# First steps reordered by hand on all engines, and the first turn of each unit with half the transposes and silu in four half-height operations

## What is computed

```python
# sandwich: x = x + layernorm(A(layernorm(x)));  x = x + layernorm(B(layernorm(x)))
h = x @ Win.T + bin                                  # 512 -> 64
for l in range(4):                                   # A: four layers on 64 features
    y = silu(layernorm(h, l1w, l1b))
    h = h + sconv(y, phazor, last_conv) * scl        # decaying complex convolution over the sequence
    y = silu(layernorm(h, l2w, l2b) @ w1.T + b1)     # 64 -> 256
    h = h + y @ w2.T + b2                            # 256 -> 64
out = layernorm(h) @ Wout.T + bout
# B: hidden + gate * (softmax over the 8 best of 128 memory slots) @ values ..., with
#    router scores (+ log_rel), a learned and a variance-based uncertainty for the gate
```

## Time and profile before

| | us |
|---|---|
| median of 3 runs | 204.45 (204.21 to 204.62) |
| the profiled execution | 204.57 |
| its span | 202.8 |
| mean granted clock of PE | 0.992 of full speed |
| HBM read, written | 10.87 MB, 4.19 MB |

### The profile page before, as it was taken

One profiled execution on the slowest core, in us unless ns is written; L12 is line 12 of the kernel. 1 busy time (PEld: TensorE's weight loads), 2 busy tenths in 40 slices (PEclk: granted clock), 3 DMA queues, 4 the chain that ended last, 5 costly groups with the idle time before them and its releaser, 6 DMA issues.

```text
span 202.8 us, 3759 instructions
## 1 busy us (share of the span) xinstructions
PE 181.9 (90%) x1210; PEld 148.8 (73%) x1210; DVE 157.4 (78%) x547; ACT 109.8 (54%) x281; POOL 84.0 (41%) x142
## 2 busy tenths in 40 slices
PE   0797996859999998999999899999999898988992
PEld 0797995758988788788998689989988444555430
DVE  6898978886588768784977776655899997998872
ACT  1595687524456467637555445462836585863210
POOL 4222269724044422343224522467462735555400
PEclk9999999978999999999999999999999999999999
DMA  5999990000000000000000000000000000002675
GB/s 158 419 376 400 417 368 14 5 0 0 0 5 0 0 3 0 0 3 0 0 0 5 0 0 0 3 0 3 2 0 2 0 3 0 2 0 105 228 283 216
DMA packets 5505, 15.31 MB, mean 75 GB/s; under 512 B 925, under 2 KB 1965, under 8 KB 4462
## 3 DMA queue, kind: packets, MB, share of 16 engines
q1 hardware_dynamic: 5486, 15.07, 19.7%
HBM read 10.87 MB, written 4.19 MB: 74 GB/s over the span
## 4 chain that ended last, share of the span: by engine, by line
PE 68%; DVE 7%; POOL 7%; DMA 6%; ACT 5%; issue 3%; SPq 2%; DVEq 0%; ACTq 0%
PE bank L1508 15%; PE bank L1400 11%; PE bank L1632 7%; PE bank L1490 6%; DMA M<-in_mraw 6%; PE bank L1464 4%; PE bank L1452 4%; POOL RS L360 4%; PE bank L1567 3%; PE bank L1638 3%; POOL M L380 2%; PE bank L1440 2%; PE bank L1556 2%; ACT XA L593 2%; DVE Z L1001 1%
## 5 line engine op out<-in xcount | busy, mean ns | idle before, releaser
L360 POOL TENSOR_TENSOR RS<-SS,nhalf 128x4 f32<-128x4 f32 x36 | 42.9, 1202 | 67.9 <-DVE SS L995 67.6
L1508 PE MATMUL bank<-ffst,HD 128*128 128x128 f32 x256 | 32.7, 283 | 0.0
L1508 PEld LDWEIGHTS bank<-ffst,HD 128*128 128x128 f32 x256 | 31.3, 200 | 0.2
L995 DVE TENSOR_REDUCE SS<-SQ 128x4 f32<-128x260 f32 x36 | 15.2, 421 | 20.9 <-ACT SQ L635 20.3
L1400 PE MATMUL bank<-M,XT 128*128 128x226 f32 x128 | 27.6, 362 | 0.1
L659 ACT ACTIVATE HD<-bank,b1r 128x512 f32<-128x512 f32 x32 | 20.3, 684 | 10.9 <-PE bank L1490 10.8
L1400 PEld LDWEIGHTS bank<-M,XT 128*128 128x128 f32 x128 | 23.2, 189 | 3.6 <-issue 3.1
L635 ACT ACTIVATE SQ<-bank 128x256 f32<-128x256 f32 x36 | 13.8, 383 | 19.6 <-PE bank L1508 9.6
L640 ACT ACTIVATE Y<-bank,cvst 128x512 f32<-128x512 f32 x16 | 12.5, 779 | 15.1 <-PE bank L1452 15.1
L1035 DVE TENSOR_TENSOR_SCAN V<-cvst,U 128x514 f32<-128x514 f32 x16 | 19.5, 1218 | 0.0
L1490 PE MATMUL bank<-Z,w1r 64*128 64x256 f32 x128 | 18.1, 402 | 0.4
(11 more groups left out here) (265 smaller groups left out, 346.0 us busy)
## 6 DMA issues: line engine op xcount, KB each, us to landing
...
```

The lines of the kernel that those rows point to most:

```text
L360: pool.tensor_tensor(RS[:, g, :], SS[:, g, :], nhalf[:, :], ALU.pow).then_inc(done, 1)
L995: dve.tensor_reduce(SS[:, g, :], SQ[:, g, :, :], AX.X, ALU.add).then_inc(done, 1)
L1508: last = pe.matmul(HK[g][:, j * P:(j + 1) * P], HD[:, u % 2, a, at:at + P], ffst[:, L, a * P:(a + 1) * P], start=False, stop=True, skip_gr ...
```

## The change

It has two parts. First, the order of the first steps is written out anew on POOL, ACT, DVE and PE (each has now a `first_steps`). SP issues chp first, c6 ahead of XT(0), and w2r behind X(2) instead of ahead of M. PE computes nine products of `ones` with itself into a spare bank before the first real one and three after it (`warm`). chp's first operations on DVE come ahead of the wait for winr. mix_columns comes behind turn1(0), setup_ffn behind column_sums; project_x(0) and (1) have banks of their own and come before hidden(0). project(0) adds b2 from the f32 row B2F at its start, where it took B2W at its end. score_rows is cut in two and moved ahead of the sums of steps 13 and 14. In setup_late(1) eight PE records (four products) become one transpose.

Second, from unit 4 to unit 15 DVE writes each tile's features once (scale in place of scale_twice, 256 columns), turn1 makes two transposes instead of four, each of two tiles side by side, and silu1 is four operations of 64 partitions x 256 columns: each half of the partitions of T1B is written to both halves of Y.

```diff
-        XPAIR = {ts[0]: ts for ts in XSTEP.values() if len(ts) == 2}
+        XPAIR = {ts[0]: ts for k, ts in XSTEP.items() if len(ts) == 2 and k >= 3}
...
         def x_bank(t):
+            if t < 2:
+                return bank[6 + t][:, 0:XW]
             at = HW if t in XSECOND else 0
             return LB[:, at:at + XW]
...
+            sp.dma_start(chp[:, :], ch).then_inc(s_ch, 16)
             sp.dma_start(winr[:, :, :], win).then_inc(s_win, 16)
             sp.dma_start(binr[:, :], binb).then_inc(s_win, 16)
-            sp.dma_start(chp[:, :], ch).then_inc(s_ch, 16)
+            sp.dma_start(c6[:, :], c64).then_inc(s_c64, 16)
...
-                if g == 0:
-                    sp.dma_start(c6[:, :], c64).then_inc(s_c64, 16)
                 if g == 1:
                     sp.dma_start(WOR[:, :], woutb).then_inc(s_m, 16)
+                    sp.dma_start(M[:, :, 0:AW], mraw).then_inc(s_m, 16)
+                if g == 2:
                     sp.dma_start(w2r[:, :], w2n).then_inc(s_w2, 16)
-                    sp.dma_start(M[:, :, 0:AW], mraw).then_inc(s_m, 16)
...
-                if s < GROUPS:
-                    norm(s, ss1, rs1)
-                if s == 2:
-                    for c in range(1, VC):
-                        centre_m(c)
-                if s + 1 < GROUPS:
-                    input_rstd(s + 1)
-                if s == 1:
-                    centre_m(0)
+            def first_steps():
+                norm(0, ss1, rs1)
+                input_rstd(1)
+                norm(1, ss1, rs1)
+                centre_m(0)
+                input_rstd(2)
+                centre_m(1)
+                norm(2, ss1, rs1)
+                centre_m(2)
+                centre_m(3)
+                input_rstd(3)
+                norm(0, ss2, rs2)
+                norm(3, ss1, rs1)
+                norm(1, ss2, rs2)
+                norm(4, ss1, rs1)
+                norm(2, ss2, rs2)
...
-            for s in range(UNITS + 1):
+            first_steps()
+            for s in range(GROUPS, UNITS + 1):
                 step(s)
...
             def silu1(u):
                 g, L = u % GROUPS, u // GROUPS
                 act.wait_ge(t1, u + 1)
-                act.activation(by_seq(Y[:, g, :])[:, :, 1:SL], by_seq(T1B[:, :]), ACT.Silu,
-                               bias=cvst[:, L, LB0:LB0 + 1], scale=cvst[:, L, LW0:LW0 + 1]).then_inc(y1, 1)
+                if u < GROUPS:
+                    act.activation(by_seq(Y[:, g, :])[:, :, 1:SL], by_seq(T1B[:, :]), ACT.Silu,
+                                   bias=cvst[:, L, LB0:LB0 + 1], scale=cvst[:, L, LW0:LW0 + 1]).then_inc(y1, 1)
+                    return
+                for lo in (0, DIM):
+                    for to in (0, DIM):
+                        at = 1 + lo // DIM * P
+                        last = act.activation(by_seq(Y[to:to + DIM, g, :])[:, :, at:at + P],
+                                              by_seq(T1B[lo:lo + DIM, 0:HW]), ACT.Silu,
+                                              bias=cvst[lo:lo + DIM, L, LB0:LB0 + 1],
+                                              scale=cvst[lo:lo + DIM, L, LW0:LW0 + 1])
+                last.then_inc(y1, 1)
...
+            def first_steps():
+                square(0, (h0_done, 1), sq1)
+                input_mean(1)
+                input_squares(GT, 2 * GT)
+                mix_rows()
+                silu1(0)
+                square(1, (h0_done, 2), sq1)
+                input_mean(2)
+                input_squares(2 * GT, 2 * GT + 2)
+                column_means()
+                input_squares(2 * GT + 2, 3 * GT)
+                silu1(1)
+                ffn_out()
+                square(2, (h0_done, 3), sq1)
+                input_mean(3)
+                input_squares(3 * GT, 3 * GT + 2)
+                square(0, (a1, 1), sq2)
+                input_squares(3 * GT + 2, 4 * GT)
+                silu1(2)
+                x_out(0)
+                square(3, (h0_done, 4), sq1)
+                x_out(1)
+                z_out(0)
+                square(1, (a1, 2), sq2)
+                silu2(0, 0)
+                silu2(0, 1)
+                silu1(3)
+                square(4, (a2, 1), sq1)
+                z_out(1)
+                square(2, (a1, 3), sq2)
+                silu2(1, 0)
+                silu2(1, 1)
...
             def step(s):
-                if s < GROUPS:
-                    square(s, (h0_done, s + 1), sq1)
                 ffn = 0 <= s - 2 < UNITS
-                if s + 1 < GROUPS:
-                    input_mean(s + 1)
-                    if s < 2:
-                        input_squares((s + 1) * GT, (s + 2) * GT)
-                if s == 1:
-                    square(0, (a1, 1), sq2)
-                if s == 2:
-                    input_squares(3 * GT, 3 * GT + 2)
-                    z_out(0)
-                    input_squares(3 * GT + 2, 4 * GT)
-                    square(1, (a1, 2), sq2)
                 if s < UNITS:
                     silu1(s)
                 else:
                     last_z(s)
-                if s == 0:
-                    ffn_out()
-                if s == 1:
-                    column_means()
-                if s >= 3:
-                    for t in XSTEP.get(s - 1, ()):
-                        x_out(t)
+                for t in XSTEP.get(s - 1, ()):
+                    x_out(t)
                 if GROUPS <= s + 1 < STEPS:
                     if 2 * GROUPS <= s + 1 < 3 * GROUPS:
                         pads_out(s + 1 - 2 * GROUPS, s - GROUPS + 2)
                     square(s + 1, (a2, s - GROUPS + 2), sq1)
-                if ffn and s >= 3:
+                if ffn:
                     z_out(s - 2)
-                if 2 <= s - 1 < UNITS:
+                if 0 <= s - 1 < UNITS:
                     square(s - 1, (a1, s), sq2)
                 if ffn:
                     silu2(s - 2, 0)
...
+            def mark(ins):
+                chain[0] += 1
+                ins.then_inc(dve_step, 1)
...
+            dve.wait_ge(s_ch, 16)
+            dve.tensor_scalar(pol[:, 0, :], chc("re"), -1.0, None, ALU.mult)
+            link(dve.tensor_scalar(pol[:, 1, :], chc("im"), -1.0, None, ALU.mult))
+            dve.tensor_tensor(pol[:, 2, :], pol[:, 0, :], chc("re"), ALU.max)
+            mark(dve.tensor_tensor(pol[:, 3, :], pol[:, 1, :], chc("im"), ALU.max))
+            mark(dve.tensor_tensor(pol[:, 4, :], pol[:, 2, :], pol[:, 3, :], ALU.max))
+            mark(dve.tensor_scalar(pol[:, 5, :], pol[:, 4, :], TINY, None, ALU.max))
...
-                link(dve.scalar_tensor_tensor(out=B2F[:, :, :], in0=rows(sm[0:ROWS, 32:32 + DEPTH], DEPTH, DIM),
-                                              scalar=-1.0 / DIM, in1=b2r[0:ROWS, :, :], op0=ALU.mult, op1=ALU.add))
+                dve.scalar_tensor_tensor(out=B2F[:, :, :], in0=rows(sm[0:ROWS, 32:32 + DEPTH], DEPTH, DIM),
+                                         scalar=-1.0 / DIM, in1=b2r[0:ROWS, :, :], op0=ALU.mult,
+                                         op1=ALU.add).then_inc(b2_mean, 1)
+                dve.wait_ge(b2_mean, 1)
                 link(dve.tensor_copy(B2W[:, :, :], B2F[:, :, :]))
...
+            def score_rests():
...
-                table_level(4, 0, 1)
+                table_level(0, 0, DEPTH)
+                table_level(1, 0, DEPTH)
+                first_h(0)
+                table_level(2, 0, DEPTH)
                 sum_squares(0, sq1, ss1)
-                table_level(5, 0, 1)
+                table_level(3, 0, DEPTH)
                 scale_twice(0)
-                table_level(6, 0, 1)
-                table_level(7, 0, 1)
+                for k in range(4, 8):
+                    table_level(k, 0, 1)
+                first_h(1)
                 modulate(0)
-                first_h(1)
-                scan(0)
                 sum_squares(1, sq1, ss1)
-                demodulate(0)
                 table_level(4, 1, 2)
                 scale_twice(1)
-                table_level(5, 1, 2)
-                sum_squares(0, sq2, ss2)
+                scan(0)
+                demodulate(0)
                 modulate(1)
                 first_h(2)
+                sum_squares(2, sq1, ss1)
+                table_level(5, 1, 2)
+                scale_twice(2)
                 scan(1)
-                sum_squares(2, sq1, ss1)
+                demodulate(1)
+                sum_squares(0, sq2, ss2)
+                ffn_means()
+                first_h(3)
                 scale(0, rs2, z2)
-                demodulate(1)
-                scale_twice(2)
-                ffn_means()
+                modulate(2)
+                sum_squares(3, sq1, ss1)
+                scale_twice(3)
                 sum_squares(1, sq2, ss2)
-                first_h(3)
-                modulate(2)
+                scan(2)
                 scale(1, rs2, z2)
-                sum_squares(3, sq1, ss1)
-                scan(2)
-                scale_twice(3)
                 demodulate(2)
```

(59 more changed lines are left out.)

24 lines of the change are left out of this document (8 added, 16 removed).

## The result

The changed kernel takes **212.44 us** (median of 4 runs, 210.25 to 212.66) against 204.33 for the kernel before beside it: ratio **1.0365, 95% interval 1.0328 to 1.0401**. It is slower by 8 us, where 199.1 was forecast with a range to 202.4. The steps are compared in stretches of profiled executions in which that clock reads 1.00.

The account below looks back on a forecast made before the run. PE (TensorE), 90% busy, was taken to bound most steps, a chain over ACT, POOL and DVE the filling. Gains of 2.7 (filling) and 2.65 us (steps) sum to 5.35, giving 199.1 us; 8-in-10 range 196.8 to 202.4.

Parts of the forecast that it names:

- With 0.10 overlap 0.46 each: silu1 in the twelve steps: four half-height operations on ScalarE take 0.46 us net each, 1.84 in all.
- the filling: Stretch before the twelve steps: the new order brings turn1(4) to 49.4 us, a gain of 2.7 us.
- Hidden at 3.40: Within a step, T being turn1's start: hidden starts 3.40 us after T, behind z_out, against 3.53 before.
- Rival 2: Twelve steps: ACT becomes their bound, silus of 0.52 to 0.55 or later x_outs; +2.8, 201.9 us; chance 13%.
- Rival 3: Twelve steps: half-height silus cost 0.68 net, deciding from 0.57 us per operation; +10.6, 209.8 us; chance 6%.
- Step 13: score_rows goes before the sum, removing PE's stall ahead of turn1(14): -0.9 and -0.3, together -1.2 us.
- Step 7: Bound by the loop from project round to turn1, from which 0.29 + 0.22 go: -0.5 us.
- Step 5: Transpose of vpT replaces eight records of 1.08 us: about -0.9; the loop allows it, at T + 5.13.
- (a): Start of the kernel: first_h(0) at 7.7 to 11.3 us, first_h(1) ends at 16.7 instead of 17.5, 0.7 gained.
- (b): From first_h(2) to turn1(3): turn1(3) at 41.3 us, or 40.8 with POOL undisturbed, instead of 42.65.
- (c): Around turn1(3) to turn1(4): PE's clock holds, project(0) takes 1.8 instead of 3.35 us; waiting on silu2(0) loses 0.6 to 0.9.
- Rival 1: Early first steps: PE's clock falls in a new gap and slows first_h(2), +2 to 2.3 us, 201.3 us; chance 12%.

Follow-up runs that it names:

- the first part alone: The kernel before with only the new order of the first steps, the moved score_rows and the transpose in setup_late(1): 203.2 us, ratio 0.9943.
- after: The whole changed kernel, both parts, against the kernel before: 212.44 us, ratio 1.0365.
- two silus: The changed kernel with the two of four half-height silus that write the other half of Y left out: 201.36 us, ratio 0.9817 to the kernel before.
- gaps filled: Twelve unread products in PE's two new idle times before turn1(0): added to the changed kernel 210.48 us; added to its first part without the second 201.47 us.

## Why the prediction was wrong, step by step

**"With 0.10 overlap 0.46 each" (the steps): the overlap was wrong.** The duration was right (0.56), the overlap of 0.10 was carried over from z_out without its condition. The text even named the gap ("No row shows an ACT operation that reads one half of the partitions and writes the other") but then asked only how much of the *duration* is fixed, while the overlap was taken as given; its sign of being wrong, too, looked at the 0.56 alone. Four silus take 2.30 us, not 1.84, so hidden is later by about 0.47. By the prediction's own threshold of 0.57 net, 0.575 an operation, with the filling's 2.7 us gained, would have been about break-even with before, not a loss of 8 us. The rest is the next step.

**"Hidden at 3.40", counted from T: a wait was missing.** The list of what PE waits for in a step had z_out and not x_out. turn2(u) writes a bank from which x_out still has to read (its wait is on xa_read), and x_out stands behind the silus. Before, x_out was done at T + 1.66 and turn2 came at T + 2.33 without an idle time, so nothing showed it; PE's timeline of before, T being 97.03:

```profile
99.36 0.38 PE L1477 MATMUL bank<-ident,Z 128*128 128x128 f32 x2
```

With the silus as forecast, x_out would have ended at T + 2.62, turn2 come at about 2.75 and hidden, 1.24 later, at T + 3.99: 0.59 of the error is this wait alone, 0.48 the missing overlap, and 3.40 + 0.59 + 0.48 = 4.47 is what was measured. The split between the two is reckoned; what a run shows is that putting x_out first gave 0.68 a step back, and 4.5 us of the 10.2 by which all steps missed. By the same account the step with x_out breaks even with before where 0.42 + 4n + 0.37 + 0.13 + 1.24 = 3.53, at n = 0.34 us an operation, and not at 0.57: an estimate, since other waits would come in.

**Rivals 2 and 3.** Rival 2 had the mechanism in part ("x_outs later than reckoned, so that hidden is later than before everywhere"), but priced it at 2.8 us. Rival 3 (slower) gave 209.8: 0.88 a step above the forecast, 10.6 in all. Steps 11, 12 and 15 came 1.05 to 1.07 above the forecast, all twelve together 10.2. That its sum is near is luck, for neither of its reasons held: not 0.68 net an operation, but 0.575 and the wait. Its 6% were too few because its threshold was reckoned without x_out. The sentence from the Trainium skill, "ScalarE: Activation LUTs", What ACT_TABLE_LOAD costs (consecutive ACTIVATEs overlap by some 93 ns), agrees with the runs for operations that keep their partitions (0.56 long, 0.46 to 0.47 apart), and with no pair that changes them (0.56 to 0.575 apart); the fixed time that it gives each operation, paid again by every part of a split, pointed the right way, though its figure is 0.585 for what took 0.561. (The prediction put the loss by that figure at about 1 us; 0.03 for each of 48 operations are 1.5.)

**Single steps.** Step 13 was forecast at -1.2 by moving score_rows: -1.06 in the first part alone, right; in after the +0.93 of its kind lies on top. Step 7, -0.5 for the loop: nothing in after, -0.48 with two silus, right as to the loop, which ScalarE took back. Step 5, -0.9: only -0.29 in the first part alone. The eight records are gone, but the step is then bound by the loop at 5.75 us, which I had put at 5.13; the two silus bring it to 5.26. Steps 11 to 15 with two silus gain 0.19, close to the 0.13 to 0.15 and the 0.22 of PE.

**The filling (-2.7): about half of it came.** (a) and (b) put turn1(3) at 41.3; with the clock held it came at 42.1 to 42.3, and at 41.5 with the first part's gaps filled. first_h(1) was to end at 16.7; in the first part alone XT(1) came at 14.0, not 13.0, and it ends at 17.9 (at 16.4 in the profile of after). There DVE's first_h(3) began at 38.27, not at 37.4, and from it to turn1(3) are 3.99 us. The prediction's own terms for this stretch, 0.8, 0.35, 0.6, 0.35, 1.0 and 0.7, are 3.8 and give 41.2 with POOL undisturbed and 42.1 beside a scan, where it wrote 40.8 and 41.3: a mistake in adding. POOL's power took 1.01. (c) was right about the clock: it stays at 1.00 and project(0) takes 2.05 us. But "the split bias with B2F costs nothing" was not:

```profile
44.27 0.69 PE L1559 MATMUL bank<-B2F,ones 1*128 1x256 f32 x2
44.89 2.05 PE L1570 MATMUL bank<-ffst,HD 128*128 128x128 f32 x16
```

It holds PE for 0.62 us ahead of project(0), where B2W's product before held it for 0.22 (46.44 to 46.66). The 0.6 to 0.9 us set aside for project(0)'s wait on silu2(0) weren't needed: silu2(0) was done at 44.47, ahead of project(0). (From the ends that it names, the prediction's 2.4 to 3.1 for this stretch would be 2.0 to 3.15, and column_sums, put at 1.8, is 2.12 in its row.) From turn1(3) to turn1(4) are 8.64 us, in each of the kernels with the first part, against 8.1 forecast and 9.45 before. Together that is -1.2 to -1.3 at a held clock, and -2.0 at most where the gaps are filled too.

**Rival 1** (the clock falls in a new gap, 12%) came true as well in the profiled execution (and by their mean clocks in two more of the four), at the place it named and with its price of 2 us: first_h(2) 2.0 us longer, turn1(4) 1.6 later, and medians lower by 2.0 and 1.7 us when the gaps were filled. I had set against it a gap before, 17.5 to 18.5, that did no harm; the new ones are 1.10 and 2.03 us.

In the sum: forecast -5.35; steps +10.2 off (7.55 instead of -2.65), filling +2.9 off at this profile's clock (+0.2 instead of -2.7), of which 1.6 is the clock.

Open: why a change of the first partition ends the overlap in ScalarE; and how much idle time PE may have before the clock falls: 1.10 and 2.03 us with 3.84 us of work between did it in the profile shown, 1.07 and 2.04 with the same work between did not in the kernel with x_out first, nor did 1.70 and 1.45 in the first part alone. Runs show single cases here, not a rule.
